# Squared norms of queries and keys: from two accumulating ScalarE passes to VectorE statistics and GpSimd products

## The reference, cut to what matters

```python
Xn = _layernorm(X, ln_g, ln_b)
QKV = jnp.einsum('bsd,ed->bse', Xn, W_in)
Q, K, V = jnp.split(QKV, 3, axis=-1)
Q = _rotary(Q, ROT)
K = _rotary(K, ROT)
A = jnp.sum(_l2norm(K) * V, axis=-2)
Y = A[:, None, :] * _l2norm(Q)
Y = jnp.einsum('bsd,ed->bse', Y, W_out)
```

## Time and profile before

| what | value |
|---|---|
| median of three runs | 1544.98 us |
| the profiled execution | 1550.83 us |
| its span, first to last instruction | 1548.9 us |
| PE busy | 1376.8 us, 89% of the span |
| ACT busy | 1149.7 us, 74% |
| DVE busy | 1135.8 us, 73% |
| POOL busy | 902.6 us, 58% |
| mean granted TensorE clock over the span | 0.961 of full speed |

### The profile page before, as it was taken

One profiled execution on the slowest core, in us unless ns is written; L12 is line 12 of the kernel. 1 busy time (PEld: TensorE's weight loads), 2 busy tenths in 40 slices (PEclk: granted clock), 3 DMA queues, 4 the chain that ended last, 5 costly groups with the idle time before them and its releaser, 6 DMA issues. The chain is left out here.

```text
span 1548.9 us, 37505 instructions
## 1 busy us (share of the span) xinstructions
PE 1376.8 (89%) x10765; PEld 1290.8 (83%) x10765; DVE 1135.8 (73%) x4170; ACT 1149.7 (74%) x4085; POOL 902.6 (58%) x1233
## 2 busy tenths in 40 slices
PE   6799999999999999999999999999994799999940
PEld 4699899898998899989999899998983798898830
DVE  4467777777777777777777777777665687787765
ACT  3588888888888888888888888888872455555535
POOL 4455666666666666666666666666544255555565
PEclk8899999999999999999999999999997799999975
DMA  3000000000000000000000000000003776777746
GB/s 91 11 11 11 17 15 17 19 15 17 15 17 19 15 17 15 17 19 15 17 15 17 19 15 17 15 17 8 10 10 59 219 238 210 220 227 219 218 148 192
DMA packets 64629, 96.24 MB, mean 62 GB/s; under 512 B 10892, under 2 KB 48786, under 8 KB 64306
## 3 DMA queue, kind: packets, MB, share of 16 engines
q1 hardware_dynamic: 44738, 71.90, 15.7%
q0 software_dynamic: 8896, 16.94, 3.2%
q10 hardware_dynamic: 10800, 5.06, 1.2%
HBM read 71.55 MB, written 23.35 MB: 61 GB/s over the span
## 5 line engine op out<-in xcount | busy, mean ns | idle before, releaser
L698 ACT ACTIVATE probs<-ps_s,neg_max 128x128 f32<-128x128 f32 x1024 | 361.7, 365 | 163.7 <-DVE neg_max L945 160.6
L513 POOL TENSOR_TENSOR probs_n<-probs,inv_sum 128x512 f32<-128x512 f32 x256 | 266.8, 1042 | 219.2 <-DVE inv_sum L951 211.7
L1367 PE MATMUL ps_s<-kvT,u_sb 128*128 128x128 f32 x2048 | 274.8, 277 | 0.8 <-issue 0.8
L1380 PE MATMUL ps_o<-value_w,tT 128*128 128x128 f32 x2048 | 260.2, 275 | 1.9 <-ACT tT L716 1.8
L1367 PEld LDWEIGHTS ps_s<-kvT,u_sb 128*128 128x128 f32 x2048 | 254.4, 191 | 7.0 <-issue 1.0
L1380 PEld LDWEIGHTS ps_o<-value_w,tT 128*128 128x128 f32 x2048 | 244.1, 192 | 2.9 <-ACT tT L716 2.9
L956 DVE TENSOR_TENSOR pT_lo<-ps_pT,pT_hi 128x512 fp32r<-128x512 f32 x256 | 175.5, 686 | 84.9 <-ACT pT_hi L707 84.9
L611 POOL DMA_INDIRECT y_rows<-wvT,f_id x144 | 145.1, 1008 | 154.7 <-DVE wvT L1284 100.2
L945 DVE TENSOR_REDUCE neg_max<-ps_s 128x4 f32<-128x512 f32 x256 | 176.9, 691 | 42.7 <-PE ps_s L1367 32.2
L698 ACT ACTIVATION_READ_ACCUMULATOR probs<-ps_s,neg_max 128x1 f32 x1024 | 207.4, 203 | 0.0
L1390 PE MATMUL ps_pT<-ident,probs_n 128*128 128x128 f32 x1024 | 157.7, 276 | 37.5 <-DVE pT_lo L956 36.6
(11 more groups left out here) (274 smaller groups left out, 3564.7 us busy)
## 6 DMA issues: line engine op xcount, KB each, us to landing
u_sb<-in_expert_w SPq DMA_DIRECT2D x45, 578.0 KB
tT<-in_expert_w SPq DMA_DIRECT2D x27, 578.0 KB
f_x<-x_rows SPq DMA_DIRECT2D x72, 130.0 KB
tT<-y_rows SPq DMA_DIRECT2D x16, 512.0 KB, 4.7
x_raw<-in_x SPq DMA_DIRECT2D x64, 64.0 KB, 1.8
c_raw<-in_ctx_in SPq DMA_DIRECT2D x64, 64.0 KB, 2.0
out<-u_sb ACTq DMA_DIRECT2D x16, 256.0 KB, 2.3
y_rows<-wvT,f_id POOLq DMA_INDIRECT x144
```

What stands on the lines that cost most here:

```text
L513: nc.gpsimd.tensor_tensor(probs_n[:, sl], probs[:, sl], inv_sum[:, sl, :].rearrange("p (u o) -> p u o", o=1).to_broadcast([P, UP, P]), ALU ...
L698: last = nc.scalar.activation(probs[:, sl, j], ps_s[sl][:, j * P:(j + 1) * P], ACT.Exp, bias=neg_max[:, sl, j:j + 1], accum_out=sums[:, sl ...
L1367: last = nc.tensor.matmul(ps_s[sl][:, j * P:(j + 1) * P], u_sb[:, c // 2, BT * p + b, h:h + 2].rearrange("p h s -> p (h s)"), kvT[:, c, 2 ...
L1380: last = nc.tensor.matmul(ps_o[:, 0:D], tT[:, (p + 1) % 2, h], value_w[:, h], start=(h == 0), stop=(h == H - 1))
```

## The change

ACT keeps the copy to `qkv` and loses the two Square passes, and with them its wait for `sq_done`. DVE reads `qkv` with two `bn_stats` ahead of the rotary turn and makes mean and variance of each with two `bn_aggr` behind it. POOL forms mean * mean + variance, the mean square, with two products of one column each ahead of its add and power. The mean square is the sum of squares over D, so eps is divided by D, and the output weights by D, since both factors come out larger by sqrt(D). In the fill the same functions are called through `rotate` and `qk_rstds`.

```diff
             def qk_rstds(j):
                 q = j % 2
+                pool.wait_ge(qk_moments, 2 * j + 2)
+                for i in range(2):
+                    nc.gpsimd.tensor_scalar(ss_qk[:, q, i:i + 1], mv_qk[:, q, i, 0:1], mv_qk[:, q, i, 0:1], mv_qk[:, q, i, 1:2],
+                                            ALU.mult, ALU.add).then_inc(sq_done, 1)
                 rstd(ss_qk[:, q], se_qk[:, q], rs_qk[:, q], eps_l2, sq_done, 2 * j + 2, qk_eps, qk_rstd, j)
...
             def keep_qkv(j):
                 q = j % 2
                 act.wait_ge(qkv_ps, j + 1)
-                act.wait_ge(sq_done, 2 * j)
                 nc.scalar.activation(qkv[:, q], A_QKV(j), ACT.Copy).then_inc(qkv_done, 1)
-                for i in range(2):
-                    nc.scalar.activation(sq_junk[:, i], A_QKV(j)[:, i * D:(i + 1) * D], ACT.Square,
-                                         accum_out=ss_qk[:, q, i:i + 1]).then_inc(sq_done, 1)
...
+            def qk_sums(j):
+                dve.wait_ge(qkv_done, j + 1)
+                for i in range(2):
+                    nc.vector.bn_stats(st_qk[:, j % 2, i], qkv[:, j % 2, i * D:(i + 1) * D]).then_inc(qk_stats, 1)
+
+            def qk_mean(j):
+                for i in range(2):
+                    dve.wait_ge(qk_stats, 2 * j + i + 1)
+                    nc.vector.bn_aggr(mv_qk[:, j % 2, i], st_qk[:, j % 2, i]).then_inc(qk_moments, 1)
...
                 if on(t, 5):
+                    qk_sums(t + 5)
                     rot_turn(t + 5)
+                    qk_mean(t + 5)
...
             def rotate(j):
+                qk_sums(j)
                 rot_turn(j)
+                qk_mean(j)
                 rot_cos_part(j)
                 rot_add(j)
```

More of the change, by code:

```diff
@@ L112, in decoder_layer @@
         qkv = sb("qkv", [P, 2, 3 * D])
-        sq_junk = sb("sq_junk", [P, 2, D])
+        st_qk = sb("st_qk", [P, 2, 2, 6])
+        mv_qk = sb("mv_qk", [P, 2, 2, 2])
         ss_qk = sb("ss_qk", [P, 2, 2])
@@ L293, in decoder_layer @@
         c_in = [sem(f"c_in{q}") for q in range(X_RING)]
-        names = """in_stats in_moments in_eps in_rstd x_hat_done c_hat_done xT_ps xnT_done qkv_ps qkv_done sq_done
+        names = """in_stats in_moments in_eps in_rstd x_hat_done c_hat_done xT_ps xnT_done qkv_ps qkv_done qk_stats qk_moments sq_done
         qk_eps qk_rstd rot_turned rot_cosed rot_done kvp_done pick_done at_ps yT_done wo_ps
@@ L302, in decoder_layer @@
         e_sum_done e_z_done e_stats e_moments e_eps e_rstd e_nm_done e_out_done""".split()
-        (in_stats, in_moments, in_eps, in_rstd, x_hat_done, c_hat_done, xT_ps, xnT_done, qkv_ps, qkv_done, sq_done,
+        (in_stats, in_moments, in_eps, in_rstd, x_hat_done, c_hat_done, xT_ps, xnT_done, qkv_ps, qkv_done, qk_stats, qk_moments, sq_done,
          qk_eps, qk_rstd, rot_turned, rot_cosed, rot_done, kvp_done, pick_done, at_ps, yT_done, wo_ps,
@@ L491, in _ @@
             nc.gpsimd.memset(eps_out[:], 4 * EPS_LN).then_inc(half_set, 1)
-            nc.gpsimd.memset(eps_l2[:], EPS_L2).then_inc(half_set, 1)
+            nc.gpsimd.memset(eps_l2[:], EPS_L2 / D).then_inc(half_set, 1)
             nc.gpsimd.memset(eps_x1[:, 0:1], EPS_LN / 4).then_inc(half_set, 1)
@@ L645, in keep_prepared @@
                     nc.scalar.activation(winT[:], bank[:, 0:3 * D], ACT.Copy).then_inc(win_kept, 1)
-                    nc.scalar.activation(woutT[:], bank[:, 3 * D:4 * D], ACT.Copy, scale=0.5).then_inc(prep_act, 1)
+                    nc.scalar.activation(woutT[:], bank[:, 3 * D:4 * D], ACT.Copy, scale=0.5 / D).then_inc(prep_act, 1)
                 elif kind == "t":
```

## The result

| | median | runs | ratio, 95% interval |
|---|---|---|---|
| before | 1546.61 us | 1544.03 to 1548.81 (4) | |
| after | 1637.95 us | 1632.84 to 1646.07 (4) | 1.06 (1.0554 to 1.0645) |
| forecast | 1629 us | range 1602 to 1674 | |

The kernel became 91 us slower. The profiled execution after took 1635.17 us with a span of 1633.3 us, 84.4 us more than before; TensorE's mean granted clock is 0.961 in both.

What follows compares the result with a forecast made beforehand. PE bounds the periods, through DVE's `row_max(0)` to `pT_lo`. 57.5 periods x 1.42 us = 81.7 us, plus 2.2 us of fill, make 84 us: 1635 us profiled, 1629 us median, range 1602 to 1674 us.

Steps and rivals of the forecast that it cites:

- The bound, the place and the order of causes: In the periods: PE waits for DVE's `pT_lo`; late aggregates delay POOL, then `k_pick`, then `row_max(0)`, by 1.42 us a period.
- The 0.20 us of room: On DVE ahead of `row_max(0)`: the idle time, waiting for PE's scores, that can absorb delay before the period grows.
- DVE's own work: Two statistics and two aggregates a tile on DVE, all ahead of `k_pick`: 0.57 us.
- The price of a product: POOL's one-column product ahead of its power: x = 0.38 us each, from bounds of 181 ns and 794 ns.
- the formula 0.66 + 2x: The us a period gains when `row_max(0)` comes late, x being one POOL product; 1.42 us at x = 0.38.
- The wait of `k_pick`: On DVE each tile: a new wait of 1.40 us for POOL's power.
- Dear products: Rival: a POOL product costs the same whatever its size, x = 0.79; 1676 to 1679 us; chance 0.18.
- ACT's relief at nothing: Dropping two Square passes frees 0.50 us a tile on ACT, but only lengthens its wait for DVE's maximum: worth nothing.
- faster* rival: The periods hang on ACT through `keep_qkv`, so each tile gives back 0.50 us: 30 us less, 1515 us; chance 0.03.
- PE's wait in `turn_queries`: PE waits some 0.7 us a period for DVE's `kv_prod`, adding nothing beyond the period's 1.42 us.
- The fill: Before the periods, two tiles whose `k_pick` already waits for POOL: 2.2 us in all, from nothing to twice that.
- The sum: Periods and fill together: 84 us more, 1635 us for an execution like the profiled one, 1629 us for the median.

Runs made afterwards that it cites:

- statistics earlier: The changed kernel with DVE's statistics and aggregates of the periods moved ahead of `row_max(3)`, fill unchanged: 1565.36 us, ratio 1.0051 to before.
- that of `seen`: The kernel before with only `seen_add` moved from ahead of the second maximum to behind `keep_pT(0)`: 1525.28 us, ratio 0.9786 to before.
- DVE's work alone: The kernel before with the change's statistics and aggregates added on DVE, results unused, Squares kept on ACT: 1557.78 us, ratio 1.0008 to before.
- the relief alone: The kernel before without ACT's two Square passes, the sums a constant, so the norms are left out: 1558.16 us, ratio 1.0001 to before.
- both moves: The changed kernel with periods' statistics ahead of `row_max(3)`, ACT's Squares kept in the fill, and `seen_add` moved later: 1527.79 us, ratio 0.9798 to before.

## Why the prediction was right, point by point

**The bound, the place and the order of causes held.** PE bounds the loop through DVE's `row_max(0)` and `pT_lo`; `k_pick` waits for POOL; what stands behind it makes `row_max(0)` late by the wait less the room. The move of the statistics and that of `seen` show it from both sides, the one without any change in work, the other without any part of the change. One reading in it was wrong: of the 66 maxima that wait for PE, 58 are `row_max(3)` and only five, in the first five periods, are `row_max(0)`; those rows don't show that `row_max(0)` waits. The 0.20 us of room, read from starts and ends, is borne out by DVE's work alone, which fits in.

**DVE's own work**, put at 0.57 us a tile, takes 0.46 where measured alone. It was rightly given the 0.26 + 0.20 us of room, which in the periods it fits by itself.

**The price of a product**, x = 0.38, was the term with the widest bounds (0.18 to 0.79). It is 0.44 on the mean and 0.42 in the period shown. With 0.42 the formula 0.66 + 2x gives 1.50 us a period; measured 1.49. The wait of `k_pick`, forecast 1.40, is 1.48; the period, 18.9, is 19.04; the 81.7 us are 86.2. Where the products run beside the row maximum (statistics earlier) the two take 0.73 us (380 ns each on the mean of that run), and beside the rotary steps 0.84, so some of the miss may be the neighbour and not the operation; I didn't try this by itself.

**Dear products** did not come true: 0.44 us on one column stands against 0.79 on 128. By the 1.03 cycles per element of the Trainium skill ("GPSIMD Engine Reference", section 3.1) nearly all of the 0.79 would be what doesn't grow with the columns, 0.68 us by my estimate; here the measurement decides, and the fixed part is at most 0.44.

**ACT's relief at nothing** held, and with it the *faster* rival fell: the relief alone is 1.0001.

**PE's wait in `turn_queries`** was forecast at 0.7 us and is 0.60. That it adds nothing beyond the period's 1.42 was right: `row_max(0)` follows DVE without idle time.

**The fill is the term that was mis-sized**: 2.2 us, from nothing to 4.4, and it is 6.5, outside its own bounds. I counted the two tiles whose `k_pick` waited before already, but the fill works five, and in after `k_pick` waits in all of them. PE's `turn_queries` of the five comes 0.45 us earlier than before in the first, and 0.44, 1.41, 2.19 and 4.55 us later in the next four. The last 2.0 us come behind the fifth, at the lower clock, and I had weighed the clock for the periods alone, where it did hold. The rows of PE in the fill, on which the prediction does not draw, show it standing for 1.49 us in the fifth tile before already.

**The sum** in the profiled pair, 84.4 us against 84, is closer than its terms by luck: periods 4.5 us over, fill 4.3 us over, and the untouched last part 8.3 us below. The medians, 1638 against 1629, give the miss its real size. PE's busy share, forecast at 89%, is 93.3%, in part since matmuls whose operands come late are longer in the profile: between 100 and 1080 us the mean of `project`'s matmuls into `ps_a` grew from 273 to 323 ns, that of `turn_queries` from 273 to 328.

## What to carry to other kernels

Work moved off an engine that idles right behind it gives nothing back, and the engine to which it goes may pay not with the work but with the place of its result: count the chain from the new producer to the consumer (here products, add, power and the hand-overs, 2.05 us from the aggregates' end) against the work that stands between the two in the consumer's order. If the chain is longer, look for an earlier place for the producer before giving the change up: two steps moved by one row maximum took the whole loss of the periods away. And count every tile of the fill too, and look there for waits of TensorE, since a stretch at the lower clock may follow.

## What the hardware showed that I had not expected

**A small VectorE instruction took 0.9 us beside GpSimd.** In before, `seen` on 128x8 has a mean of 771 ns, and 154 when moved. Groups of before:

```profile
L1021 DVE TENSOR_TENSOR seen<-seen,mask 128x8 bf16<-128x8 bf16 x64 | 49.3, 771 | 0.0
```

The neighbour is POOL's multiply. Timelines of before, POOL and DVE:

```profile
622.71 1.03 POOL L513 TENSOR_TENSOR probs_n<-probs,inv_sum 128x512 f32<-128x512 f32 x1
```

```profile
617.71 0.96 DVE L1014 TENSOR_TENSOR mask<-picked 128x8 bf16<-128x8 f32 x1
...
622.85 0.91 DVE L1021 TENSOR_TENSOR seen<-seen,mask 128x8 bf16<-128x8 bf16 x1
```

`seen` starts 0.14 us into the multiply and ends 0.02 us after it (623.76 against 623.74); both of its inputs are in SBUF. `mask`, just as small and with its inputs in SBUF too, does the same with the multiply before, which ends at 618.65; it ends at 618.67. Over all of before, 55 of 64 `seen` and 60 of 64 `mask` start inside such a multiply, and each ends 0.02 to 0.09 us behind it; the other 13 take 0.14 to 0.19 us. The Trainium skill has this ("SBUF — State Buffer", section "Who interferes with whom"): a VectorE instruction with two SBUF inputs contends with a GpSimd instruction that reads SBUF, and of the ports that the two share it says that the lock is exclusive. The trace agrees for the long multiply; beside POOL's short products in after (648.80 to 649.64) the rotary step of 648.98 keeps its 0.29 us. So it is not only semaphore waits that tie these two engines together, other than the description of the kernel says. `mask` has a mean of 910 ns and stands between `k_pick` and `row_max(0)`; no run moved it, so what that would be worth is open.

**The clock fell behind one idle stretch.** 2.85 us of idle PE, from 61.6 us on, were followed by 10 us at 1.2 GHz, 1.49 us at the same place before were not; in the periods waits of 0.6 to 0.7 us twice in 19 us leave it at 2.4 GHz. The length of this wait alone does not settle it. With both moves it was 1.48 us, ending at 59.75 us, and the clock was still 1.00 from 62 to 64 us but 0.57 on the mean of the next 4 us (window of that run):

```profile
64.00:68.00 4.00, 3.86 (x19) 3.86 (x20) 2.33 (x11) 2.02 (x9) 2.13 (x5) 0.57 0.11 33
```

With the statistics earlier it was 2.85 us again, and the clock was still 1.00 from 64 to 66 us and 0.50 only from 68 us on. What decides is open here.

**The same kernel differs by 0.8% between sessions:** before took 1546.6 us beside after, and 1558.3 and 1558.8 us beside the experiments, on two chips. That is more than the fill is worth, and can only be met with ratios. In the profiles the difference lies behind the periods: with ACT's relief alone fill and periods end at 1092.51 us against 1093.37 before, and what follows takes 463.2 us against 455.5. Its cause is open.
